# A graph-attention merge moved from a stage of its own into the loop over edge tiles

## The chip, the cores and the metric

The kernel runs on one NeuronCore of one Trainium2 chip. The metric is the device time of one execution in microseconds (us). The engines are TensorE (PE, with its weight loads PEld), VectorE (DVE), ScalarE (ACT), GpSimd (POOL) and SyncE (SP, which here only issues DMAs). Each runs its own instruction stream; semaphores order them.

## The reference, cut to what matters

Four graph layers with residual connections run over 3125 nodes of 128 features and 103125 edges, sorted by destination. The change is in the third layer, a two-head graph attention (GAT). For each edge e from src to dst and each head h:

```
z      = xl[src, h] + xr[dst, h]                  # xl = n @ Wl + bl, xr = n @ Wr + br, 128 features per head
score  = sum_f att[h, f] * leaky_relu(z[f], 0.2)
a      = exp(score - max over the edges of dst)   # softmax over the edges that end in dst
out    = sum_e a * xl[src, h]  /  (sum_e a + 1e-16)
```

The heads are then averaged and a residual projection is added. The softmax is over all edges of a destination, and these can lie in two or more edge tiles, so each tile computes with its own maximum and the tiles have to be merged: the sums of a tile are multiplied by exp(its maximum - the final or running maximum) before they are added.

## The kernel before, in words

**Tiles.** The edges lie in 202 tiles of 512, each of 4 groups (SUB) of 128. The destinations of a tile fall into a window of WIN = 20 consecutive nodes that begins at a base read at run time from `k.base_i`.

**The loop.** `attend` (L1991) serves two layers: the additive attention (`gat` false) and the GAT layer (`gat` true). `over_tiles` (L78) writes each engine's stream as a software pipeline of `(lag, stage)` pairs: in step s the engine does `stage` for tile s - lag. The ring of buffers has 8 slots in the GAT layer and 12 in the additive one; `head` rounds are written out ahead of the hardware loop, and a tail behind it. In a GAT step:

- GpSimd (L2088 to L2092) issues for tile n, once `sums_ready` says that tile n - 8 is summed, four indirect DMAs (`gather`, L894) of 128 rows of `table2` (1 KB each). Behind each gather stands a memset of a scratch tile `pause` of 128 x 280 fp16 (L905), which first waits for the memset before it. This stream is written out in full, without a hardware loop.
- TensorE does `scores` of tile s-3, `features` of s-1 (which wait for each gathered group), `turn_sums` of s-6, `turn_top` and `turn` of s-4, and `sums` of s-5.
- ScalarE does `raise_scores` (the exp) of s-3, `activate` of s-1 and `copy_sums` of s-5.
- VectorE does `tops` (the maximum per node, head and tile) of s-3, `onehots` of s, `keep_sums` of s-6 (the sums of the tile into its own strip of `k.partial`), `leaky` of s-1, `best_of_nodes` of s-4 and `edge_weights` of s-4. `best_of_nodes` (L2269) reads the window's base with `window_base` (L913, a register load from SBUF), copies the tile's maxima into `k.rows`, and keeps the maximum by node in `k.node_top` with one more instruction.
- SyncE loads the destination rows and the windows of `parts2`, two tiles at a time (L2080).

**The merge.** Behind the loop `merge_gat` (L2303) is a stage of its own, over groups of 24 tiles (`over_groups`, L1095): VectorE and GpSimd subtract the final maximum by node from each tile's maxima (L2324), ScalarE raises them (L2387), TensorE spreads the factors over 128 lanes and collects the sums of the weights by node (L2400, L2402), VectorE scales the kept sums (L2362) and adds each tile's 128 x 40 strip to `k.acc` at its window (L2374), and GpSimd adds the 2 x 20 sums of weights to `k.node_sum` (L2415). `divide_gat` (L2474) follows. Each stage ends with its semaphores cleared and a barrier.

Around the GAT layer, `project` (L561) clears `k.node_sum` and `k.node_top` just before the loop.

## Time and profile before

| | us |
|---|---|
| median of 3 runs (4847.73 to 4849.36) | 4847.86 |
| the profiled execution, its own time | 4848.75 |
| its span | 4847.0 |
| its mean granted TensorE clock, share of full speed | 0.854 |

The engines' busy shares of the whole span are PE 83%, PEld 47%, DVE 60%, ACT 36% and POOL 72%. They are averages over all layers; the stages that matter here are two stretches of the GAT layer, given as rows below. In the rows, a line number is one of the kernel before; a `q` behind an engine (POOLq, DVEq) marks its sequencer, whose register and load instructions do not count as busy. The time of TensorE's records is partly modelled.

### The profile page before, as it was taken

How to read it: one execution, taken by the hardware profiler on the slowest of the kernel's cores; microseconds unless marked ns; L12 is line 12 of the kernel's file. 1: busy time of each engine (PE TensorE's matmuls, PEld its weight loads, DVE VectorE, ACT ScalarE, POOL GpSimd, SP SyncE). 2: the span in 40 equal slices, each digit the busy share in tenths (PEclk: the TensorE clock that was granted, in tenths of full speed). 3: DMA queues.
4: the chain of work that ended last, by engine and by line, in shares of the span. 5: the costliest groups of instructions: out<-in, count | busy, mean ns of one | idle time of the engine just before them, and what ended most of it. 6: DMA issues, size and time to landing. Idle time of an engine off the chain costs nothing. (4 is left out here: it accounts for less than half of the span.)

```text
span 4847.0 us, 91319 instructions
## 1 busy us (share of the span) xinstructions
PE 4013.8 (83%) x22566; PEld 2268.5 (47%) x22566; DVE 2916.2 (60%) x8457; ACT 1759.0 (36%) x4474; POOL 3476.2 (72%) x4676
## 2 busy tenths in 40 slices
PE   3997948888888887578888888885399999999986
PEld 1344434445445445344444444442255566666652
DVE  7995043333333334656666666666688888888868
ACT  3774033344444444433333333331322222222217
POOL 0522358888888884688888888884278888888862
PEclk8998957676777767788888888886699999999999
DMA  2333522222222221333333333330066666666650
GB/s 80 86 86 97 163 68 59 56 57 57 57 57 57 57 57 33 110 100 98 99 99 99 99 99 99 99 96 9 29 101 104 104 105 105 105 104 105 104 109 14
DMA packets 377438, 402.52 MB, mean 83 GB/s; under 512 B 86457, under 2 KB 322502, under 8 KB 377030
## 3 DMA queue, kind: packets, MB, share of 16 engines
q0 software_dynamic: 151904, 198.72, 21.2%
q1 hardware_dynamic: 225382, 202.21, 14.8%
q8 instruction: 43, 0.70, 0.1%
q14 instruction: 109, 0.89, 0.1%
HBM read 312.91 MB, written 87.78 MB: 83 GB/s over the span
## 5 line engine op out<-in xcount | busy, mean ns | idle before, releaser
L1727 POOL DMA_INDIRECT sums<-gathered,idx x606 | 989.1, 1632 | 217.1 <-issue 168.5
L899 POOL DMA_INDIRECT gathered<-table,sources x952 | 912.3, 958 | 216.9 <-issue 154.7
L1589 PE MATMUL bank<-wide 128*128 128x512 bf16 x3636 | 851.4, 379 | 0.0
L2247 DVE TENSOR_REDUCE neg_raw<-bank 80x1 f32<-80x512 f32 (+1 forms) x404 | 277.5, 687 | 632.5 <-DMA dst_pair<-local_rows 192.3
L905 POOL MEMSET pause<- 128x280 f16 x1616 | 579.0, 358 | 0.4
L899 POOL DMA_INDIRECT wide<-table,sources x464 | 443.4, 956 | 106.6 <-issue 73.7
L1589 PEld LDWEIGHTS bank<-wide 128*128 128x128 bf16 x3636 | 347.7, 98 | 364.1 <-issue 1.7
L2197 ACT ACTIVATE msg<-bank,neg_top 80x512 f32<-80x512 f32 (+1 forms) x404 | 275.9, 683 | 544.5 <-DVE neg_top L2249 365.4
L1228 POOL TENSOR_TENSOR acc<-acc,msg 128x20 f32 x404 | 172.4, 427 | 350.7 <-issue 187.9
L2107 PEld LDWEIGHTS bank<-ident,gathered 128*128 128x128 f32 x1360 | 193.9, 167 | 281.0 <-issue 226.6
L2128 PE MATMUL bank<-zact,att_cells 128*80 128x512 f32 x404 | 317.5, 880 | 0.1
L2209 ACT COPY partial<-bank 32x20 f32 (+1 forms) x808 | 134.3, 166 | 480.5 <-remote 243.1
L2265 DVE COPY edge_rows<-bank 128x320 f32<-128x320 f32 (+1 forms) x404 | 183.2, 454 | 202.9 <-remote 91.4
L2240 DVE TENSOR_TENSOR zact<-zact,bank 128x512 f32<-128x512 f32 x404 | 259.5, 683 | 63.9 <-ACT zact L2189 41.5
L1175 DVE TENSOR_SCALAR gathered<-iota_c,partial 128x500 f16<-128x500 f16 x808 | 277.2, 377 | 7.9 <-PE bank L1184 6.1
L2107 PE MATMUL bank<-ident,gathered 128*128 128x128 f32 x1360 | 248.2, 321 | 40.7 <-DMA gathered<-table,sources 18.1
L2125 PE MATMUL bank<-zact,att_cells 128*32 128x512 f32 x808 | 266.9, 733 | 0.1
L1184 PE MATMUL bank<-gathered,zact 128*128 128x500 f16 x812 | 209.8, 381 | 57.2 <-ACT zact L1291 35.8
L2189 ACT ACTIVATE zact<-bank 128x512 f32<-128x512 f32 x404 | 218.8, 593 | 76.5 <-DMA window<-parts 47.9
L2138 PE MATMUL bank<-ident,msg 80*128 80x80 f32 (+1 forms) x1616 | 217.8, 264 | 33.1 <-issue 23.2
L1495 DVE TENSOR_SCALAR onehot_t<-dst_pair,iota_w,always 128x512 bf16<-128x512 bf16 x481 | 218.3, 454 | 19.5 <-DMA dst_pair<-local_rows 17.0
L2163 PE MATMUL bank<-edge_rows,gathered 128*128 128x80 f32 x1088 | 190.8, 333 | 45.8 <-issue 24.3
(407 smaller groups left out, 7803.8 us busy)
## 6 DMA issues: line engine op xcount, KB each, us to landing
zact<-in_src_flat SPq DMA_DIRECT2D x202, 192.0 KB
edge_rows<-in_attr_rows SPq DMA_DIRECT2D x202, 128.0 KB
dst_pair<-local_rows SPq DMA_DIRECT2D x177, 128.0 KB
gathered<-table,sources POOLq DMA_INDIRECT x952
dst_pair<-local_rows SPq DMA_DIRECT2D x202, 64.0 KB
counts<-wide SPq DMA_DIRECT2D x4, 3000.0 KB
counts<-fm_ab SPq DMA_DIRECT2D x4, 3000.0 KB
fm_ab<-counts SPq DMA_DIRECT2D x4, 3000.0 KB, 11.2
```

What stands on the lines that cost most here:

```text
L899: pool.indirect_dma_start(out=g[:, j, :], out_offset=None, in_=table, in_offset=bass.IndirectOffsetOnAxis(ap=mine, axis=0)).then_inc(rows_ ...
L905: pool.memset(k.pause[:, :], 0.0).then_inc(paused, 1)
L1175: hot = dve.tensor_scalar(k.cell_hot[slot][:, j, :], k.iota_c[:, :], own, None, ALU.is_equal)
L1589: pe.matmul(k.bank[b][:, :], k.split[t.two][:, c, :], k.source_hot[t.two][:, b * CHUNK:(b + 1) * CHUNK], start=first, stop=c == PARTS - 1, ...
L1727: pool.indirect_dma_start(out=k.sums[j], out_offset=bass.IndirectOffsetOnAxis(ap=k.idx[t.slot][:, j:j + 1], axis=0), in_=out_rows(t)[:, j, ...
L2107: pe.matmul(z_bank(t, h)[:, j * P:(j + 1) * P], g[:, j, h * F:(h + 1) * F], k.ident[:, :], is_transpose=True, start=(j == 0), stop=False, ...
L2125: mm = pe.matmul(score_bank(t)[own_cells(h), :], a.att[h][:, own_cells(h)], k.zact[t.two][:, h, :], start=False, stop=True, skip_group_che ...
L2128: mm = pe.matmul(score_bank(t), a.att[0][:, :], k.zact[t.two][:, 0, :], start=False, stop=True)
L2189: act.mul(k.zact[t.two][:, h, :], z_bank(t, h)[:, :], 0.2).then_inc(slope_ready, 1)
L2197: act.activation(raised(t), score_bank(t), ACT.Exp, bias=k.neg_top[lanes(t), bass.ds(t.t, 1)], accum_out=k.weight_sum[lanes(t), bass.ds(t. ...
L2240: m = dve.tensor_tensor(za, za, z_bank(t, h)[:, :], ALU.max)
L2247: dve.tensor_reduce(raw, score_bank(t), AX.X, ALU.max, negate=True).then_inc(top_found, 1)
```

## The change

1. `merge_gat` and its helpers are taken out. A class `WindowMerge` is added, and its steps are put into the GAT loop.
2. In `best_of_nodes` VectorE no longer copies the maxima to `k.rows` and takes the maximum. `note` writes (tile maximum - running best of the node) into a strip, and then updates the running best. TensorE's `turn_top` waits for this one count in place of two.
3. For every four tiles (BATCH) VectorE makes two factors per tile and node out of the noted difference d: min(-d, 0) for the old sums and min(d, 0) for the new ones (`lower`); ScalarE raises both with one exp (`raise_factors`); TensorE spreads them over the lanes and sums the weights by node (`spread_factors`, into bank 7 ahead of `turn_sums`); VectorE takes them out and scales the kept sums of the four tiles (`take`).
4. GpSimd, 17 tiles behind its own gathers, scales and adds: behind the four gathers of tile n it does for tile m = n - 17 one instruction each, `scale_rows` (2 x 20), `scale_acc` (128 x 40), `add_rows` (2 x 20), `add_acc` (128 x 40). The base of tile m's window is read into a register ahead of tile n's first gather.
5. The memset behind each gather of the GAT layer is 128 x 70 fp16 (`k.breath`); that of the additive layer stays at 280, and lies in `k.fb`.
6. Behind the last step come a tail for the last two batches, and the adds of the last six tiles on VectorE. `head` is 2 on TensorE and ScalarE and 3 on VectorE, where it was 1.
7. `node_top` and `node_sum` change partitions (32 to 33 and 0 to 1), and the two memsets that clear them change places in the list. GpSimd's stream waits once, at its start, for the bases.

```diff
-    k.node_top = k.fa[0:HEADS2, :]
-    k.sum_lanes = slice(32, 32 + HEADS2)
+    k.node_top = k.fa[32:32 + HEADS2, :]
+    k.sum_lanes = slice(0, HEADS2)
...
-    k.pause = k.sb("pause", [P, PAUSE], FP16)
+    k.pause = k.fb[:, 0:PAUSE // 2].bitcast(FP16)
+    k.breath = k.wide[:, 0, 512:512 + PAUSE // 8].bitcast(FP16)
...
+def rest(k, pool, paused, t, j, columns):
+    if t.t + j > 0:
+        pool.wait_ge(paused, t.t * SUB + j)
+    pool.memset(columns, 0.0).then_inc(paused, 1)
...
+class WindowMerge:
+    MERGED, FRONT = 17, 64
...
+    def note(self, dve, t, top, at):
+        half, i = t.slot // BATCH, t.slot % BATCH
+        best = self.k.node_top[:, bass.ds(at, WIN)]
+        wait_count(dve, self.best, t.t)
+        dve.tensor_tensor(self.raised_tops[half][:, i * WIN:(i + 1) * WIN], top, best,
+                          ALU.subtract).then_inc(self.noted, 1)
+        dve.wait_ge(self.noted, t.t + 1)
+        return dve.tensor_tensor(best, best, top, ALU.max).then_inc(self.best, 1)
+
+    def scale_acc(self, eng, m, at):
+        half, i = m % self.ring // BATCH, m % BATCH
+        wait_count(eng, self.acc_added, m)
+        w = self.k.acc[:, :, bass.ds(at, WIN)]
+        eng.tensor_tensor(w, w, self.spread[half][:, :, i * WIN:(i + 1) * WIN], ALU.mult).then_inc(self.acc_scaled, 1)
+
+    def add_acc(self, eng, m, at):
+        eng.wait_ge(self.acc_scaled, m + 1)
+        w = self.k.acc[:, :, bass.ds(at, WIN)]
+        eng.tensor_tensor(w, w, self.a.partial[:, :, m, :], ALU.add).then_inc(self.acc_added, 1)
...
+    def beside_gathers(self, pool, n, at, j):
+        m = n - self.MERGED
+        if not 0 <= m < self.k.tiles:
+            return
+        if j == 0:
+            pool.wait_ge(self.taken, self.done(m // self.ring, m % self.ring // BATCH))
+            self.scale_rows(pool, m, at)
+        elif j == 1 and m < self.pooled():
+            self.scale_acc(pool, m, at)
+        elif j == 2:
+            self.add_rows(pool, m, at)
+        elif j == 3 and m < self.pooled():
+            self.add_acc(pool, m, at)
...
+    def lower(self, dve, g, half):
+        dve.tensor_tensor(self.cell_sums[half][:, 0:n * WIN].rearrange("p (t n) -> p t n", n=WIN),
+                          k.weight_sum[:, bass.ds(first, n)].unsqueeze(2).to_broadcast([self.a.lanes, n, WIN]),
+                          place, ALU.mult)
+        dve.wait_ge(self.noted, first + n)
+        d = self.raised_tops[half][:, 0:n * WIN]
+        dve.tensor_scalar(self.factors[half][:, 0:n * WIN], d, -1.0, 0.0, ALU.mult, ALU.min)
+        dve.tensor_scalar(self.factors[half][:, wide:wide + n * WIN], d, 0.0, None,
+                          ALU.min).then_inc(self.lowered, 1)
+
+    def take(self, dve, g, half, bank, kept):
+        wait_count(dve, self.acc_scaled, first + n - self.ring)
+        dve.tensor_copy(self.spread[half][:, :, 0:n * WIN], old)
+        dve.wait_ge(kept, first + n)
+        dve.tensor_tensor(p, p, new, ALU.mult)
+        wait_count(dve, self.rows_added, first + n - self.ring)
+        dve.tensor_copy(self.row_factors[half][:, 0:n * WIN], self.factors[half][:, 0:n * WIN])
+        dve.tensor_tensor(self.row_sums[half][:, 0:n * WIN], self.factors[half][:, wide:wide + n * WIN],
+                          bank[0:self.heads, self.FRONT + 4 * wide:self.FRONT + 4 * wide + n * WIN],
+                          ALU.mult).then_inc(self.taken, 1)
...
+                if gat:
+                    pool.wait_ge(lo.limited, 1)
+                    for n in range(k.tiles + fold.MERGED):
+                        at = fold.window_of(pool, n)
+                        if n < k.tiles:
+                            t = Tile(n, n % ring, n // ring)
+                            wait_count(pool, sums_ready, n + 1 - ring)
+                            pool.sem_inc(gathers_begun, 1)
+                        for j in range(SUB):
+                            if n < k.tiles:
+                                gather_rows(k, pool, table, rows(t), rows_loaded, t, j)
+                                rest(k, pool, paused, t, j, k.breath)
+                            fold.beside_gathers(pool, n, at, j)
+                    pool.wait_ge(fold.rows_added, k.tiles)
...
-                    dve.tensor_copy(k.rows[0:heads, bass.ds(t.t * WIN, WIN)], top_bank(t)).then_inc(top_kept, 1)
-                    wait_count(dve, best, t.t)
-                    m = k.node_top[:, bass.ds(at, WIN)]
-                    dve.tensor_tensor(m, m, top_bank(t), ALU.max).then_inc(best, 1)
+                    fold.note(dve, t, top_bank(t), at)
...
-def merge_gat(k):
...
-            late=[(k.node_sum, 0.0), (k.node_top, -NEAR)])
+            late=[(k.node_top, -NEAR), (k.node_sum, 0.0)])
...
-        merge_gat(k)
```

## Rows read from the trace of the kernel before

**Rows 1.** By stretch: length; busy PE, PEld, DVE, ACT, POOL; clock; DMA share; GB/s

```profile
2017.00:3282.00 1265.00, 1057.68 (x7487) 566.11 (x7487) 765.49 (x1975) 417.88 (x995) 1057.29 (x1616) 0.87 0.35 99
3304.20:3431.50 127.30, 44.38 (x54) 11.22 (x54) 76.35 (x345) 5.18 (x9) 67.42 (x298) 0.50 0.00 1
```

**Rows 2.** Groups on POOL, 2050 to 3280 us: busy, mean ns | idle before, releasers

```profile
L899 POOL DMA_INDIRECT gathered<-table,sources x391 | 374.1, 957 | 102.7 <-issue 56.8 <-DMA wide<-table,sources 45.8 <-PE bank L2159 0.2
L905 POOL MEMSET pause<- 128x280 f16 x785 | 281.0, 358 | 0.2
L899 POOL DMA_INDIRECT h_nm<-table,sources x200 | 191.3, 957 | 47.8 <-issue 29.1 <-DMA wide<-table,sources 18.7
L899 POOL DMA_INDIRECT wide<-table,sources x194 | 185.4, 956 | 52.9 <-issue 29.8 <-DMA wide<-table,sources 23.2
```

**Rows 3.** Timeline (start, duration us, engine, line, [idle before]) around a stop of POOL

```profile
2614.91 0.95 POOL L899 DMA_INDIRECT h_nm<-table,sources  x1 [0.17 <-issue]
2615.86 0.35 POOL L905 MEMSET pause<- 128x280 f16 x1
2616.34 0.26 ACT L2203 COPY tile_rows<-bank 64x128 f32<-64x128 f32 x1 [3.78 <-DMA wide<-table,sources]
2617.09 0.96 POOL L899 DMA_INDIRECT gathered<-table,sources  x1 [0.88 <-DMA wide<-table,sources]
```

**Rows 4.** Timeline, TensorE's scores of two steps after POOL's last gather

```profile
3283.88 0.40 PE L2120 MATMUL bank<-onehot_t,far 64*64 64x512 bf16 x1
3288.32 0.40 PE L2120 MATMUL bank<-h_nm,far 64*64 64x512 bf16 x1
```

**Rows 5.** Additive layer: POOL's gathers, 800 to 1850 us; two scores after its last gather

```profile
L899 POOL DMA_INDIRECT gathered<-table,sources x465 | 445.2, 957 | 89.3 <-issue 76.0 <-PE bank L2163 7.8 <-remote 5.5
L899 POOL DMA_INDIRECT wide<-table,sources x234 | 223.6, 956 | 47.7 <-issue 38.1 <-PE bank L2163 6.0 <-remote 3.7
...
1897.12 0.41 PE L2120 MATMUL bank<-onehot_t,far 64*80 64x512 bf16 x1
1900.55 0.41 PE L2120 MATMUL bank<-zact,far 64*80 64x512 bf16 x1
```

**Rows 6.** Groups on POOL by form: the memsets whose width is nearest to 70

```profile
L347 POOL MEMSET far<- 64x80 bf16 x1 | 0.2, 155 | 0.0
L348 POOL MEMSET far<- 64x64 bf16 x1 | 0.1, 142 | 0.0
```

**Rows 7.** POOL: small two-operand instructions, a run of 24 subtracts, register loads

```profile
L1228 POOL TENSOR_TENSOR acc<-acc,msg x404: 219/226/68965, 167.7 to 610.6; 128x20 f32 x135
...
L676 POOL TENSOR_TENSOR gathered<-gathered,h_nm 128x128 f32<-128x128 f32 x1 | 0.4, 427 | 1.4 <-ACT h_nm L656 1.4
...
3306.03 5.22 POOL L2324 TENSOR_TENSOR wide<-wide,fm_ab 2x20 f32<-2x20 f32 x24 [24.45 <-issue]
...
L1191 POOLq TENSOR_LOAD <-base_i x152: 316/322/1049, 166.5 to 3429.8; - x152
```

**Rows 8.** POOL and VectorE beside each other (min/median/max ns; timeline; group; timeline)

```profile
L2324 POOL TENSOR_TENSOR wide<-wide,fm_ab x96: 210/221/808, 3306.0 to 3400.5; 2x20 f32<-2x20 f32 x48, - x48
...
3307.28 0.64 DVE L2294 TENSOR_TENSOR msg<-weight_sum,place 128x480 f32<-128x480 f32 x1
...
L2254 DVE TENSOR_SCALAR top_cells<-place,neg_top 64x20 f32<-64x20 f32 x197 | 100.7, 511 | 22.6
...
3298.55 0.24 DVE L2254 TENSOR_SCALAR top_cells<-place,neg_top 64x20 f32<-64x20 f32 x1
```

**Rows 9.** Groups on VectorE in the loop, and on VectorE and TensorE in the merge stage

```profile
L2247 DVE TENSOR_REDUCE neg_raw<-bank 64x1 f32<-64x512 f32 x198 | 136.3, 689 | 258.9 <-DMA dst_pair<-local_rows 192.3 <-PE bank L2125 66.0
...
L2362 DVE TENSOR_TENSOR partial<-partial,bank 128x480 f32<-128x480 f32 (+2 forms) x18 | 10.4, 618 | 0.3
...
L2400 PE MATMUL bank<-wide,head_row 2*128 (+2 forms) x36 | 30.2, 990 | 67.0 <-ACT wide L2387 67.0
```

**Rows 10.** Timeline, eight of the last adds of the merge stage

```profile
3427.84 2.63 DVE L2374 TENSOR_TENSOR acc<-acc,partial 128x40 f32 x8 [0.87 <-DVE partial L2362]
```

More of the change, by code:

```diff
@@ L223, in load_everything @@
     k.spot = k.sb("spot", [P, 3 * SUB])
-    k.node_top = k.fa[0:HEADS2, :]
-    k.sum_lanes = slice(32, 32 + HEADS2)
+    k.node_top = k.fa[32:32 + HEADS2, :]
+    k.sum_lanes = slice(0, HEADS2)
     k.node_sum = k.fa[k.sum_lanes, :]
-    k.rows = k.wide[:, :, :].rearrange("p a n -> p (a n)")[:, 0:T * WIN]
     k.best = k.sb("best", [1, 2 * HEADS1])
@@ L891, in gathered, with gather_rows, gather @@
         "p (j f) -> p j f", f=width)
-def gather(k, pool, table, g, gathers_begun, rows_loaded, t, paused=None):
+def gather_rows(k, pool, table, g, rows_loaded, t, j):
+    mine = k.sources[:, t.t * SUB + j:t.t * SUB + j + 1]
+    pool.indirect_dma_start(out=g[:, j, :], out_offset=None, in_=table,
+                            in_offset=bass.IndirectOffsetOnAxis(ap=mine, axis=0)
+                            ).then_inc(rows_loaded[t.slot][j], 16)
+def rest(k, pool, paused, t, j, columns):
+    if t.t + j > 0:
+        pool.wait_ge(paused, t.t * SUB + j)
+    pool.memset(columns, 0.0).then_inc(paused, 1)
+def gather(k, pool, table, g, gathers_begun, rows_loaded, t, paused):
     pool.sem_inc(gathers_begun, 1)
     for j in range(SUB):
-        mine = k.sources[:, t.t * SUB + j:t.t * SUB + j + 1]
-        pool.indirect_dma_start(out=g[:, j, :], out_offset=None, in_=table,
-                                in_offset=bass.IndirectOffsetOnAxis(ap=mine, axis=0)
-                                ).then_inc(rows_loaded[t.slot][j], 16)
-        if paused:
-            if t.t + j > 0:
-                pool.wait_ge(paused, t.t * SUB + j)
-            pool.memset(k.pause[:, :], 0.0).then_inc(paused, 1)
+        gather_rows(k, pool, table, g, rows_loaded, t, j)
+        rest(k, pool, paused, t, j, k.pause)
 def gather_sems(st, ring=RING):
@@ L2069, in attend @@
         paused = st.sem("paused")
-        cells_ready, top_turned, top_kept, best = (st.sem("cells_ready"), st.sem("top_turned"),
-                                                   st.sem("top_kept"), st.sem("best"))
+        cells_ready, top_turned = st.sem("cells_ready"), st.sem("top_turned")
         lo = Locals(st)
         merge = None if gat else RunningMerge(k, st)
+        fold = WindowMerge(k, st, ring) if gat else None
         with st.block() as block:
@@ L2088, in _ @@
             def _(pool):
-                for n in range(k.tiles):
-                    t = Tile(n, n % ring, n // ring)
-                    wait_count(pool, sums_ready, n + 1 - ring)
-                    gather(k, pool, table, rows(t), gathers_begun, rows_loaded, t, paused)
+                if gat:
[12 more added lines that the diff above has]
+                    pool.wait_ge(fold.rows_added, k.tiles)
+                else:
+                    for n in range(k.tiles):
+                        t = Tile(n, n % ring, n // ring)
+                        wait_count(pool, sums_ready, n + 1 - ring)
+                        gather(k, pool, table, rows(t), gathers_begun, rows_loaded, t, paused)
             @block.tensor
@@ L2174, in _ @@
                     over_tiles(pe, k.tiles, [(3, scores), (1, features), (6, turn_sums), (4, turn_top), (4, turn),
-                                             (5, sums)], ring=ring)
+                                             (5, sums)], head=2, ring=ring)
+                    fold.tail_spreads(pe)
                 else:
@@ L2216, in _ @@
                 if gat:
-                    over_tiles(act, k.tiles, [(3, raise_scores), (1, activate), (5, copy_sums)], ring=ring)
+                    over_tiles(act, k.tiles, [(3, raise_scores), (1, activate), (5, copy_sums)], head=2, ring=ring)
+                    fold.tail_raise(act)
                 else:
@@ L2281, in keep_sums @@
                                         "p (z c) -> p z c", z=heads)[:, :, 0:WIN]).then_inc(kept, 1)
+                    fold.behind_keeping(dve, t)
                 if gat:
                     over_tiles(dve, k.tiles, [(3, tops), (0, onehots), (6, keep_sums), (1, leaky),
-                                              (4, best_of_nodes), (4, edge_weights)], ring=ring)
+                                              (4, best_of_nodes), (4, edge_weights)], head=3, ring=ring)
+                    fold.tail_takes(dve, kept)
                 else:
```

217 lines of the change are left out of this document (109 added, 108 removed).

## The prediction, on record before the changed kernel ran

> **What bounds the kernel now.** I read four views, in this order. Busy time by stretch shows the two parts of the GAT layer that the change touches [rows 1]: 1265 us of loop with gathers (202 tiles), in which TensorE, the engine with the most work beside GpSimd, is busy 84% at a granted clock of 0.87, and 127.3 us of merge stage, in which no engine is busy more than 60% and TensorE stands at 0.50. The merge is plain serial time behind the loop: nothing else runs beside it.
>
> The groups on POOL say what paces the loop [rows 2]. 785 gathers are 196.25 tiles. Their busy time is 374.1 + 281.0 + 191.3 + 185.4 = 1031.8 us and the idle time before them 203.6 us, so a tile takes 6.295 us on POOL. Its own cadence is 4 x (0.957 gather + 0.358 memset + 0.165 from a memset to the next gather, which a row of the timeline prints as 0.17 [rows 3] and as many others as 0.16) = 5.92 us. The remaining 0.375 us per tile are stops: POOL waits for the sums of the tile 8 back. In the timeline such a stop costs 0.88 us from the end of the memset to the next gather, of which 0.165 would be there anyway, though what it waited for had come after some 0.13 us: ScalarE, released by the same sums, starts at 2616.34, the memset ended at 2616.21 [rows 3]. So a stop is mainly a restart of POOL's queue, about 0.75 us.
>
> Is it TensorE that is late? Once POOL has issued its last gather, two steps of the loop are 3288.32 - 3283.88 = 4.44 us apart [rows 4]. TensorE, ScalarE and VectorE together need 4.44 us for a tile, POOL 5.92. The loop is bound by POOL, and the stops come from TensorE's results arriving late while POOL runs. The additive layer has the same POOL stream with less on the other engines: a step without gathers takes 3.43 us, and over 699 gathers the idle time is 137.0 us, 0.124 us per tile above 4 x 0.165 [rows 5]. I read from this pair how the stops grow with the load of the others: 0.124 at 3.43/5.92 = 0.58, 0.375 at 4.44/5.92 = 0.75.
>
> **The change part by part.** All sums are made against the profiled execution, 4848.75 us (span 4847.0 and 1.75 around it); the median of the runs is 0.9 below that.
>
> *The merge stage goes.* From 3304.2 to 3431.5, -127.3 us [rows 1]. The stretch runs from the stage's first instruction to its last; the change of stages behind it stays.
>
> *POOL's stream in the loop.* Per gather the memset of 280 fp16 (0.358) becomes one of 70: between 0.142 (64 wide) and 0.155 (80 wide) [rows 6], I take 0.147. One two-operand instruction is added behind each. Not overlapped, 2 x 20 costs 0.221 [rows 8] and 128 x 40 costs 0.263, interpolated between 0.226 at 20 and 0.427 at 128 columns [rows 7], and the short gap to the one before it could be 0.06. Overlapped it costs less: 24 independent subtracts of 2 x 20 took 5.22 us, or, since a 0.81 us one is among them, (5.22 - 0.81) / 23 = 0.19 each [rows 7, 8]. All waits in this stream are for things done a gather or more before (scale at gathers 0 and 1, add at 2 and 3, the factors batches earlier), so I count none. A tile then costs on POOL at least 4 x (0.957 + 0.147 + 0.165) + 2 x 0.19 + 2 x 0.23 = 5.92, as now, and at most 5.08 + 4 x 0.06 + 2 x 0.22 + 2 x 0.263 = 6.28. I take the middle, 6.10, since the added instructions are independent of the memset but carry run-time addresses and counts. The register load of the window's base, one per tile (0.32 [rows 7]), I take as hidden: in the run of 24 subtracts such loads are issued while the engine works and leave no hole.
>
> *The stops.* The others' step grows by TensorE's part: two matmuls on 2 x 160 and one on 128 x 80 per four tiles. The merge stage did 202 tiles' worth of the first kind in 30.2 us at half clock [rows 9], twice that width is 60.4 / 202 = 0.30 per tile, 0.17 at clock 0.87, and with the third 0.2. The ratio becomes 4.64 / 6.10 = 0.76, practically today's, so I leave the stops at 0.38. The tile then takes 6.10 + 0.38 = 6.48 us against 6.295: +0.185 x 202 = +37 us.
>
> *VectorE and ScalarE in the loop.* `note` is two small instructions for two. Per four tiles `lower` adds three and `take` four: with the multiply of the kept sums at 160 columns for 480 in 0.618 (about 0.3) and the small ones at 0.2, some 1.6 us, 0.4 per tile, with the extra hand-offs 0.5. VectorE is busy 765.5 / 202 = 3.8 us per tile and idle 258.9 us before `tops` alone [rows 1, 9]; 4.3 of 6.48 leaves it off the path. If that cover were gone (VectorE in the chain of every step), the price is the 0.5 us, 100 us in all; below nothing it cannot go. ScalarE gets one small exp per four tiles and is busy a third of the time: nothing. The clears, the partitions and the moved scratch tiles: same sizes, nothing. POOL's wait for the bases at its start stands ahead of the first gather; what is queued behind it are all gathers, but the first features wait longer for the destination rows: nothing.
>
> *The tail.* Behind the last step: three small VectorE instructions at 0.2 (0.6), the exp (taken as 0.3), three matmuls (0.8: 0.99 at 480 columns [rows 9], a third of that each), two `take` (2.3), register loads (two at 0.32 [rows 7], 0.7), 12 dependent scale and add steps at 2.63 / 8 = 0.33 (4.0) [rows 10], four hand-offs at 0.3 (1.2), and POOL's row sums of the last tiles slightly behind: +11 us, between 8 and 18.
>
> **Sum:** -127.3 + 37 + 11 = -79 us: 4769.5 for the profiled run, 4769 for the median. With POOL's two ends (0 and +0.36 us per tile) 4732 and 4805.
>
> **A page against the trace.** VectorE's `top_cells` takes 0.511 us in the loop and 0.24 once POOL is idle, and one subtract of POOL took 0.808 for a median of 0.221, beginning at about the time of a 0.64 us VectorE multiply that reads two SBUF tiles [rows 8]: the two do hold each other up. The Trainium skill's page "SBUF — State Buffer", section "SBUF: two separate sides", says that VectorE and GpSimd share one pair of ports by an exclusive lock, taken by a VectorE operation with two SBUF inputs only against a GpSimd operation that reads SBUF. A memset reads nothing, the added instructions do, so by the rule the change pays more often than the memset did; it is the second rival.
>
> **Rivals.**
>
> 1. *The stops vanish.* If the added instructions let TensorE's results through as well as the longer memset did, and POOL's slower cadence lets them arrive in time, a tile costs 6.10: (6.10 - 6.295) x 202 = -39, in all 4848.7 - 127.3 - 39 + 11 = 4693. For it: 0.124 in the lighter layer. Against it: the ratio is no better than now.
> 2. *The port.* VectorE's `top_cells` (0.51 [rows 8]) and its one-hots, which I take at the same length, are 1.0 of 6.3 us per tile, so 16% of 4 instructions are hit, 0.64 per tile, each for up to 0.6 and on average 0.25 to 0.4, about 0.2 us: +43, 4812. Against it: L1228, beside a VectorE that is busy throughout, has a median of 0.226 and a minimum of 0.219 [rows 7].
> 3. *POOL's queue runs dry at every tile's first gather* (slower). The base's load and the wait for the sums both stand ahead of it; if the sequencer cannot run ahead past three instructions per gather, each tile pays a restart of 0.75 and the load's 0.32, 1.07 in place of 0.375: 6.10 + 1.07 - 6.295 = 0.875 x 202 = +177, 4909. It decides for slower from (127.3 - 11) / 202 = 0.576 us per tile. For it: 0.88 us per restart [rows 3], at every second tile already. Against it: no hole in the run of 24.
> 4. *It doesn't do what it says*: the instructions behind the gathers wait for `taken`. At gather n the batch of tile n - 17 must be taken; it is at step 12 behind the batch's first tile, and POOL runs at most some 3 steps ahead of that step count, so two steps are left. If not, the loop runs as in 3.
>
> **How the numbers follow.** Forecast (4732 to 4805) 0.50; stops gone or POOL cheaper still (below 4732) 0.15; the port or a VectorE in the chain in part (4805 to 4838) 0.15; within 0.2% (9.7 us, about what a measurement can tell from no change) 0.05; rival 3 and what lies near it 0.15. Faster 0.80, same 0.05, slower 0.15. The range 4700 to 4860 leaves out about a third of the second case and four fifths of the last, 0.17.
>
> **What the profile after would show.** The stretch between the last `keep_sums` and the next stage falls from 128 to some 11 us. On POOL, the 70-wide memset takes 0.15, the added instructions 0.19 to 0.26, gathers stay at 0.957; idle before gathers, less 4 x 0.165, is near 0.38 us per tile. The gather loop is about 1300 us long. Wrong if: the idle before a tile's first gather is near 1 us in every tile (rival 3); POOL's small instructions have means above 0.35 (rival 2); or POOL is seldom stopped and the loop is still above 6.5 us per tile, which would put VectorE in the chain.

## The result and the profile after

| | before | after |
|---|---|---|
| median of the runs, us | 4848.61 (4847.73 to 4858.41, 4 runs) | 4763.19 (4760.65 to 4772.97, 4 runs) |
| profiled execution, us | 4848.75 | 4760.65 |
| its span, us | 4847.0 | 4758.9 |
| mean granted TensorE clock | 0.854 | 0.861 |

The change makes the kernel faster: ratio 0.9819, 95% interval 0.9806 to 0.9832. The forecast was 4769 us, 6 us above the median.

Where the time went is read best by cutting both traces at the same events. The four stretches below are, in this order: the gathers of the additive layer (first to last), what lies between them and the first gather of the GAT layer, the gathers of the GAT layer, and what lies between its last gather and the first gather of the next layer (that contains the merge stage before, and the new tail after). Columns as in [rows 1]. The kernel before:

```profile
672.40:1883.40 1211.00, 1009.60 (x4123) 591.58 (x4123) 415.30 (x1254) 482.06 (x1461) 1056.05 (x1615) 0.72 0.22 58
1883.40:2016.90 133.50, 77.15 (x369) 56.76 (x368) 88.57 (x259) 65.83 (x152) 39.02 (x29) 0.74 0.18 63
2016.90:3280.30 1263.40, 1057.62 (x7487) 566.11 (x7487) 765.35 (x1974) 417.72 (x994) 1056.11 (x1615) 0.87 0.35 99
3280.30:3525.70 245.40, 111.22 (x502) 56.79 (x502) 150.81 (x553) 54.31 (x126) 84.46 (x314) 0.63 0.07 20
```

The changed kernel:

```profile
666.50:1878.50 1212.00, 1010.39 (x4135) 589.66 (x4136) 418.56 (x1258) 482.77 (x1468) 1058.11 (x1615) 0.72 0.22 58
1878.50:2006.70 128.20, 72.47 (x365) 55.09 (x363) 88.08 (x255) 64.70 (x148) 39.05 (x29) 0.74 0.19 66
2006.70:3303.90 1297.20, 1096.73 (x7766) 594.06 (x7764) 789.70 (x2303) 425.00 (x1041) 1063.87 (x2353) 0.86 0.34 97
3303.90:3437.60 133.70, 73.28 (x471) 49.83 (x472) 81.97 (x246) 50.29 (x120) 29.24 (x73) 0.73 0.13 35
```

The loop is 33.8 us longer, what follows it 111.7 shorter: -77.9 us. The other 10.2 us of the profiled pair lie outside the GAT layer: -5.9 ahead of the additive layer's gathers (they start at 672.4 and 666.5), +1.0 in them, -5.3 behind them. Is that the change? The experiments answer it, below.

The fifth number, POOL's busy time, is the surprise of the table: 1056.1 before, 1063.9 after, although 738 instructions were added (2353 for 1615). POOL in the loop, 2125 to 3300 us, for comparison with [rows 2]:

```profile
L897 POOL DMA_INDIRECT gathered<-table,sources x366 | 357.5, 977 | 97.7 <-issue 52.4 <-DMA wide<-table,sources 45.4
L897 POOL DMA_INDIRECT wide<-table,sources x184 | 180.0, 978 | 47.6 <-issue 28.0 <-DMA wide<-table,sources 19.5
L897 POOL DMA_INDIRECT h_nm<-table,sources x184 | 179.7, 977 | 50.3 <-issue 27.9 <-DMA wide<-table,sources 22.4
L906 POOL MEMSET wide<- 128x70 f16 x733 | 131.4, 179 | 0.5
L2051 POOL TENSOR_TENSOR acc<-acc,partial 128x40 f32 x184 | 52.0, 283 | 0.0
L2046 POOL TENSOR_TENSOR acc<-acc,wide 128x40 f32 x183 | 51.7, 282 | 0.0
L2057 POOL TENSOR_TENSOR fm_ab<-fm_ab,wide 2x20 f32 x183 | 39.4, 215 | 0.0
```

The memset's mean is 179 ns, not the 147 I took, and a gather's 977, not 957. But the added instruction begins 0.11 us behind the start of the memset, while that still runs (in another trace of the same kernel, shown further down, a memset at 2601.58 and the instruction at 2601.69), so of 179 ns about 110 count.

VectorE in the loop, 2050 to 3280 us (answers to [rows 8, 9]; L2107 and L2110 are the two wide instructions of `take`), and TensorE's new matmuls in the same stretch:

```profile
L2464 DVE TENSOR_REDUCE neg_raw<-bank 64x1 f32<-64x512 f32 x192 | 132.0, 688 | 167.3 <-DMA dst_pair<-local_rows 115.6 <-PE bank L2339 49.2 <-issue 0.6
...
L2471 DVE TENSOR_SCALAR top_cells<-place,neg_top 64x20 f32<-64x20 f32 x192 | 51.2, 267 | 22.0
...
L2107 DVE COPY wide<-bank 128x160 f32<-128x160 f32 x46 | 14.9, 325 | 101.3 <-DMA wide<-table,sources 51.4 <-PE bank L2385 40.5 <-POOL acc L2046 5.7
L2110 DVE TENSOR_TENSOR partial<-partial,bank 128x160 f32 (+1 forms) x46 | 14.5, 315 | 0.0
```

```profile
L2130 PE MATMUL bank<-wide,head_row 2*128 2x160 f32 x184 | 37.6, 324 | 3.6 <-ACT tile_rows L2418 3.5 <-issue 0.2
...
L2133 PE MATMUL bank<-wide,own 128*2 128x80 f32 x92 | 14.1, 235 | 0.0
```

TensorE got (37.6 + 14.1) / 184 tiles = 0.28 us per tile (46 batches of four tiles, by the count of L2107); VectorE's busy time in the loop rose by 24.3 us in all.

The 33.8 us of the loop are not spread evenly. Up to the 101st gather (tile 25) the kernel before takes 153.9 us and the changed one 164.4, 10.5 more, for 12% of the tiles; the rest takes 1109.5 and 1132.8 us, 0.13 us more per tile. In that first part POOL comes to tile 8, the first that has to wait for the sums of another tile, and stops once for long:

```profile
2062.22 0.95 POOL L897 DMA_INDIRECT gathered<-table,sources  x1 [11.51 <-PE bank L2372]
```

No gather of the kernel before waits even 2 us. The prediction has no term for this start.

The end of the stage, in three stretches (from the last gather until the last tile's sums are kept, the tail, and until the next stage's first instruction), and the two rows of the timeline that bound the last:

```profile
3303.90:3329.30 25.40, 23.70 (x209) 14.14 (x210) 18.57 (x63) 9.55 (x26) 10.82 (x47) 0.93 0.07 12
3329.30:3336.70 7.40, 2.24 (x12) 1.45 (x11) 4.26 (x24) 0.27 (x1) 2.64 (x12) 0.54 0.01 2
3336.70:3343.80 7.10, 0.00 (x0) 0.00 (x0) 0.01 (x1) 0.00 (x0) 0.00 (x0) 0.50 0.00 0
```

```profile
3336.51 0.20 DVE L2051 TENSOR_TENSOR acc<-acc,partial 128x40 f32 x1
...
3343.85 2.39 PE L2573 MATMUL bank<-ident,fm_ab 2*128 2x2 f32 x21 [12.31 <-PEq L933]
```

In the last 7.1 us every engine is idle. In the trace's full record POOL is in the drain that ends its block from 3336.21 on, for 5.78 us, so some 5.3 of the 7.1 are this drain. Before, it began that drain (7.23 us long) at 3280.2, beside its last gather and under the other engines' last tiles, and it cost nothing.

### The profile page after: what moved, and what is told of

The parts are those of the page before. It is cut to its first block and busy times, and to the rows that moved or that the text cites. A ratio compares the mean times of both kernels' runs of the same rounds, so it can differ in the third digit from the quotient of the medians.

```text
span 4758.9 us, 92081 instructions
## 1 busy us (share of the span) xinstructions
PE 4013.0 (84%) x22818; PEld 2281.2 (48%) x22818; DVE 2878.2 (60%) x8482; ACT 1762.1 (37%) x4516; POOL 3367.1 (71%) x5174
## 5 line engine op out<-in xcount | busy, mean ns | idle before, releaser
L1237 POOL TENSOR_TENSOR acc<-acc,msg 128x20 f32 x404 | 108.9, 270 | 408.3 <-issue 245.0
L906 POOL MEMSET fm_ab<- 128x280 f16 x808 | 290.5, 360 | 0.2
L1184 DVE TENSOR_SCALAR gathered<-iota_c,partial 128x500 f16<-128x500 f16 x808 | 258.8, 341 | 2.0 <-issue 1.6
L897 POOL DMA_INDIRECT h_nm<-table,sources x200 | 195.0, 975 | 55.3 <-issue 29.7
L1649 ACT COPY gathered<-bank 128x437 f32<-128x437 f32 x202 | 106.1, 525 | 336.7 <-PE bank L1624 249.6
```

The lines of the kernel that those rows point to most:

```text
L897: pool.indirect_dma_start(out=g[:, j, :], out_offset=None, in_=table, in_offset=bass.IndirectOffsetOnAxis(ap=mine, axis=0)).then_inc(rows_ ...
L906: pool.memset(columns, 0.0).then_inc(paused, 1)
L1184: hot = dve.tensor_scalar(k.cell_hot[slot][:, j, :], k.iota_c[:, :], own, None, ALU.is_equal)
```

## The experiments

They ran in three sets, each on another chip, and the kernel before took 4900, 4725 and 4909 us in them. So kernels are compared within a set, by their ratio to the kernel before in the same set. The first and the third set are close (the kernel without the added instructions took 4836 and 4833 us in them) and are read together, with care: the ratio of that kernel is 0.9872 in one and 0.9848 in the other, so a step of 0.24% between kernels of the two sets can be the sets alone. The changed kernel had 0.9795 (0.9781 to 0.9808) in the second set and 0.9820 (0.9805 to 0.9834) in the third.

| kernel | set | us | ratio to before (95%) | GAT gathers, us | POOL's stops in them, us |
|---|---|---|---|---|---|
| before | 3 | 4910 | 1.0002 (0.9994 to 1.0011) | 1295.8 | 106 |
| changed | 3 | 4818 | 0.9820 (0.9805 to 0.9834) | 1321.5 | 122 |
| TensorE's spreads twice | 3 | 4827 | 0.9836 (0.9823 to 0.9849) | 1329.3 | 130 |
| no added POOL instructions | 3 | 4833 | 0.9848 (0.9835 to 0.9862) | 1341.3 | 291 |
| memset 280 wide | 1 | 4841 | 0.9885 (0.9866 to 0.9904) | 1351.9 | 5 |
| no memset | 1 | 4827 | 0.9846 (0.9829 to 0.9862) | 1328.7 | 215 |
| before, memset 70 wide | 1 | 4935 | 1.0063 (1.0046 to 1.0080) | 1324.6 | 279 |
| changed | 2 | 4627 | 0.9795 (0.9781 to 0.9808) | 1196.2 | 1.5 |
| TensorE's spreads twice | 2 | 4630 | 0.9798 (0.9784 to 0.9811) | 1198.0 | 1.3 |
| one more VectorE instruction | 2 | 4631 | 0.9802 (0.9788 to 0.9815) | 1200.0 | 1.2 |
| rows on VectorE in the tail | 2 | 4621 | 0.9779 (0.9766 to 0.9793) | 1197.5 | 1.4 |

The last column is the length of the gathers less POOL's busy time in them less 808 x 0.165, the short gap ahead of a gather that nothing stops. By the same sum the first pair has 74 us of stops before and 100 after.

Counted in the traces, as gaps over 0.4 us ahead of a gather, the stops are these. In the first pair 95 of 0.78 us on average (over 0.165) became 102 of 0.99; in the third set 99 of 1.06 became 103 of 1.20. Most of the growth is at the start: up to the 101st gather the stops sum to 6 and 24 us in the first pair, 9 and 27 in the third set. Behind it they are 68 and 76 us, and 96 and 96. One long stop at tile 8 (10.0 to 11.5 us over the 0.165) stands in every trace of the first pair and of the first and third set in which the memset of the GAT layer is short or left out; it is absent where the memset is long, and in the second set.

**The long memset back.**

```
-    k.breath = k.wide[:, 0, 512:512 + PAUSE // 8].bitcast(FP16)
+    k.breath = k.wide[:, 0, 512:512 + PAUSE // 2].bitcast(FP16)
```

> The changed kernel with its memset behind each gather of the GAT layer back at 128 x 280 fp16; nothing else is different. Theory (the loop follows GpSimd's stream): of the 70-wide memset 0.131 us show per gather now, of one of 280 wide about 0.36, so a tile costs GpSimd 4 x 0.21 = 0.84 us more, 165 us over the loop; some of the 0.4 us of stops per tile goes. Between 4845 and 4926, I take 4900, so the move of the merge alone would have made the kernel slower. Rival (the loop follows VectorE or TensorE, and GpSimd has slack): only what the longer memset costs VectorE's instructions with two SBUF inputs comes back, about 0.25 us per tile, 4810. In both cases the mean of VectorE's top_cells (0.267 now, 0.511 before) goes back to 0.5 if it is the memset's length that holds it up; if it stays at 0.27, something else in the change did that.

Measured: 0.9885, which is 0.65% above the changed kernel of set 3, or 0.4% if the 0.24% between the sets is taken off: 20 to 32 us. The loop is POOL-bound to the last: no stops, 1351.9 us. For a kernel before of 4849 us, which the expectation had in mind, that would be 4793, below both figures. POOL's stream grew by 148 us (1213.6 for 1065.8), and of that 117 were paid by stops that went. The 4900 was wrong, and so was the sentence that the move alone would lose: with the long memset kept it still gains 1.15%. `top_cells` did not go back to 0.5 either:

```profile
L2471 DVE TENSOR_SCALAR top_cells<-place,neg_top 64x20 f32<-64x20 f32 x168 | 48.9, 291 | 19.3
```

**The kernel before with the short memset.**

```
-            pool.memset(k.pause[:, :], 0.0).then_inc(paused, 1)
+            pool.memset(k.pause[:, 0:columns], 0.0).then_inc(paused, 1)
...
-                    gather(k, pool, table, rows(t), gathers_begun, rows_loaded, t, paused)
+                    gather(k, pool, table, rows(t), gathers_begun, rows_loaded, t, paused, PAUSE // 4 if gat else PAUSE)
```

> The kernel before with the memset of the GAT layer at 70 fp16 wide and the merge still a stage of its own. Theory: GpSimd's own cadence falls from 5.92 us per tile by 4 x 0.18 to 0.21 to about 5.15, and its stops grow from 0.375 to 0.6 to 0.8 us, since the others need 4.44 us: the tile takes 5.85 in place of 6.295, 90 us less, 4760. Rival (every microsecond that GpSimd's stream gives up comes back as restarts of its queue, because TensorE's results reach it only when it pauses): 4848, no change. If the port between GpSimd and VectorE was what the long memset cost, top_cells falls from 0.511 to below 0.3 here too.

Measured: 1.0063, slower. The first experiment against my reading of the loop: POOL's stream lost 145 us (912.1, for 1056.9 in the third set's trace of before), the stops grew by 174, to 171 of 1.65 us on average. The loop row, with the clock at 0.84 for 0.86, and `top_cells`, which did fall:

```profile
2040.60:3365.20 1324.60, 1099.63 (x7470) 576.51 (x7472) 721.80 (x1969) 405.64 (x994) 912.05 (x1615) 0.84 0.33 95
```

```profile
L2254 DVE TENSOR_SCALAR top_cells<-place,neg_top 64x20 f32<-64x20 f32 x171 | 45.1, 264 | 19.8
```

What held `top_cells` up was not the memset beside it. In the steady loop of the first trace of before all 161 of its instructions above 0.4 us (of 188) begin while a gather runs on POOL, and 160 of them end with it to within 10 ns; the 24 that begin outside a gather take 0.28 us on average. Two of them from the third set's trace of before, the first inside a gather, the second inside a memset that began at 2601.56, then one from the kernel with the short memset, as far into a gather as the first:

```profile
2607.51 0.95 POOL L899 DMA_INDIRECT gathered<-table,sources  x1 [1.14 <-DMA wide<-table,sources]
2607.93 0.53 DVE L2254 TENSOR_SCALAR top_cells<-place,neg_top 64x20 f32<-64x20 f32 x1
...
2601.71 0.23 DVE L2254 TENSOR_SCALAR top_cells<-place,neg_top 64x20 f32<-64x20 f32 x1
```

```profile
2607.91 0.95 POOL L899 DMA_INDIRECT h_nm<-table,sources  x1 [1.63 <-DMA wide<-table,sources]
2608.33 0.23 DVE L2254 TENSOR_SCALAR top_cells<-place,neg_top 64x20 f32<-64x20 f32 x1
```

With the short memset 8 of 190 are above 0.4 us. Why the memset's length decides whether the gather ahead of it holds VectorE up is not shown.

So the short memset by itself loses 0.6%, and beside the added instructions it gains 0.4 to 0.65%.

**No memset where an added instruction stands.**

```
-                                rest(k, pool, paused, t, j, k.breath)
+                                if n < fold.MERGED:
+                                    rest(k, pool, paused, t, j, k.breath)
```

> The changed kernel without the memset wherever an added instruction stands behind the gather (from tile 17 on). Theory (the added instruction is breath enough): 4 x 0.131 = 0.52 us per tile of GpSimd's stream go, 0.2 come back as stops, -0.3 x 185 = -60 us, 4700. Rival (without a memset the results of TensorE get through late, and GpSimd is stopped with a full restart of 0.75 us in every tile): 6.40 - 0.52 - 0.4 + 0.9 = 6.4 us per tile, 4761 or more.

Measured: 0.9846 for 0.9820, two intervals that overlap, in two sets; the loop is 7 us longer than the changed kernel's of the third set. The theory (60 us less) fell; no gain or a small loss is what came, as the rival had it.

**No added instructions.** The four instructions of POOL became bare increments of their counts; the merged sums and the sums of weights are left out for the tiles that POOL handles.

```
-        pool.tensor_tensor(z, z, self.row_factors[half][:, i * WIN:(i + 1) * WIN],
-                           ALU.mult).then_inc(self.rows_scaled, 1)
+        pool.sem_inc(self.rows_scaled, 1)
```

> The changed kernel with the four instructions per tile that GpSimd does for the merge left out (the scaling and adding of the sums of the GAT layer for the tiles up to 196, and of the sums of weights, are left out; the counts are still posted). Theory (GpSimd paces the loop): 4 x 0.18 to 0.23 us of its stream go, stops grow by some 0.2 to 0.3, the tile takes 5.9 in place of 6.4 us, -95 us, 4665. Rival (VectorE or TensorE paces): 4760, unchanged. A GpSimd loop of 5.28 us own cadence that still takes 6.4 would be the sign of the rival.

> GpSimd's four added instructions per tile left out (the scaling and adding of the sums of the GAT layer for the tiles up to 196, and of the sums of weights), once more. Two paces: at a clock above 0.92 the loop falls from 5.92 us per tile towards 5.6 (the other engines' chain at that clock), -40 to -100 us; at 0.88 within 20 us of the changed kernel; at 0.85 not faster, and up to 30 us slower, which its first run hinted at (0.9872 on a chip where the changed kernel itself was not run). GpSimd alone paces: -0.7 us per tile on any chip, -140 us.

Measured: 0.9872 and 0.9848, the second beside the changed kernel: 15.6 us slower than with them. The loop rows of the third set say what happened: first the changed kernel, then the one without the instructions.

```profile
2039.90:3361.40 1321.50, 1122.71 (x7766) 592.50 (x7764) 781.08 (x2303) 423.28 (x1040) 1065.77 (x2354) 0.88 0.33 95
```

```profile
2038.00:3379.30 1341.30, 1130.74 (x7765) 603.20 (x7764) 775.92 (x2303) 423.60 (x1040) 916.62 (x1614) 0.85 0.32 94
```

POOL does 149 us less and stops 184 times for 1.61 us on average, the loop takes 20 us more, and TensorE, with the same 7765 matmuls, is busy 8 us longer at a clock of 0.85 for 0.88. Here GpSimd is not the pace.

**The changed kernel in another set.**

> The changed kernel itself once more, so that the others are compared with it on one chip: 0.982 of the time before. In the first four experiments the kernel before took 4900 us, not 4849, and the additive layer's gathers 1230 us in place of 1212, so traces are compared between kernels of one chip only. If the gather loop of the GAT layer is 1325 us where before takes 4900 us, the short memset and the added instructions of GpSimd were worth the differences that the four showed; if its mean TensorE clock differs too, that is named.

Measured: 4627 us, 0.9795. Its loop takes 1196 us, not 1322, with the same instructions, and there it is POOL that paces: 1.5 us of stops, and TensorE waits for gathered rows. The row of the loop, and TensorE's first use of the rows (last column), 2025 to 3150 us:

```profile
1971.90:3168.10 1196.20, 1063.48 (x7838) 558.96 (x7836) 806.93 (x2329) 432.95 (x1051) 1061.42 (x2354) 0.93 0.36 105
```

```profile
L2321 PE MATMUL bank<-ident,gathered 128*128 128x128 f32 x755 | 130.1, 290 | 58.2 <-DMA gathered<-table,sources 56.0
```

In the third set the same line waits for nothing, and TensorE waits for ScalarE's copy of the sums instead (2125 to 3250 us):

```profile
L2321 PE MATMUL bank<-ident,gathered 128*128 128x128 f32 x688 | 108.3, 296 | 8.7 <-issue 8.0
...
L2385 PE MATMUL bank<-ident,tile_rows 64*128 64x64 f32 x172 | 42.9, 249 | 65.0 <-ACT tile_rows L2418 57.0 <-issue 7.3
```

The clock column differs: 0.93 and 0.88 of 2.4 GHz over the loop. It does not order all the traces, though: the changed kernel's first one has 0.86 and a loop of 1297.2 us, the third set's 0.88 and 1321.5. The transfers are not what differs: from its start on POOL to its last packet a gather takes 2.44 us (median) in both sets. In a timeline the clock has two levels, 2.4 and 1.2 GHz. The same two groups of a tile (16 matmuls of the sums, 4 of the scores) in the second set:

```profile
2601.40 1.07 PE L2372 MATMUL bank<-h_nm,edge_rows 128*32 128x128 f32 x16
...
2602.73 1.05 PE L2339 MATMUL bank<-zact,att_cells 128*32 128x512 f32 x4
```

and in the third, in a tile at the lower level, with POOL's overlap beside it:

```profile
2599.73 1.92 PE L2372 MATMUL bank<-h_nm,edge_rows 128*32 128x128 f32 x16
...
2601.58 0.17 POOL L906 MEMSET wide<- 128x70 f16 x1
...
2601.69 0.29 POOL L2046 TENSOR_TENSOR acc<-acc,wide 128x40 f32 x1
...
2602.14 1.92 PE L2339 MATMUL bank<-zact,att_cells 128*32 128x512 f32 x4
```

**TensorE's spreads twice.**

```
-        for h in range(self.heads):
+        for h in [h for _ in range(2) for h in range(self.heads)]:
```

> The changed kernel with TensorE's two matmuls that spread the factors done twice in every batch of four tiles (36.1 us over 176 tiles in the trace, 0.205 us per tile). Theory that I now hold, since neither leaving out GpSimd's additions nor its memset made the loop shorter: the loop is paced by TensorE and by the hand-offs to and from it, and GpSimd's stream has slack. Then all of it shows: 0.205 x 202 = +41 us, a ratio of 0.9905 to before against 0.982. Rival (the theory of the prediction, GpSimd paces): 0 to +5 us, 0.982 to 0.983. A half of it would mean that the two take turns.

> TensorE's spreading matmuls twice (0.205 us per tile), once more, beside the next kernel, which takes the load off GpSimd. Two paces: at a clock above 0.92 nothing (as in the first run of it, +0.03%), at 0.88 or lower +20 to +45 us. GpSimd alone paces: nothing on any chip.

Measured: +2.4 us in the second set (0.9798 for 0.9795: nothing), +9.4 us in the third (0.9836 for 0.9820; the intervals overlap). TensorE's busy time in the loop rose by 43 and 42 us. So my second theory, that TensorE and the hand-offs pace the loop and all of it shows, fell as well: where POOL paces, nothing shows, and where it doesn't, about 8 of 42 us (with the ends of the two intervals, anything from nothing to half). The clock fell with it, 0.93 to 0.90 and 0.88 to 0.85. The row of the second set:

```profile
1978.00:3176.00 1198.00, 1106.56 (x8028) 603.92 (x8029) 791.63 (x2328) 430.51 (x1051) 1063.41 (x2354) 0.90 0.36 105
```

**One more VectorE instruction.**

```
+                    if gat:
+                        dve.tensor_tensor(k.wide[:, 0, 600:728], k.ident[:, :], k.ident[:, :], ALU.max)
```

> The changed kernel with one more VectorE instruction per tile behind the copy of the weights: the maximum of two SBUF inputs of 128 x 128 into a scratch tile that nobody reads; I put it at 0.2 to 0.35 us. Theory (VectorE has slack, as the prediction said): 0 to +10 us. Rival (VectorE is in the chain of every step): +40 to +70 us. Rival of the shared port: GpSimd's instructions become longer by the lock, means of 0.28 and 0.215 us rise above 0.3, and the time by some 20 us.

Measured: +3.7 us (0.9802 for 0.9795), for 43 us more of VectorE's busy time: it has slack in this set, as predicted. POOL's instructions hardly changed. First the changed kernel of that set, then this one:

```profile
L2046 POOL TENSOR_TENSOR acc<-acc,wide 128x40 f32 x182 | 52.6, 289 | 0.0
...
L2057 POOL TENSOR_TENSOR fm_ab<-fm_ab,wide 2x20 f32 x182 | 38.8, 213 | 0.0
```

```profile
L2046 POOL TENSOR_TENSOR acc<-acc,wide 128x40 f32 x181 | 54.8, 303 | 0.0
...
L2057 POOL TENSOR_TENSOR fm_ab<-fm_ab,wide 2x20 f32 x181 | 39.0, 216 | 0.0
```

**POOL through earlier.** VectorE scales and adds the row sums of the last six tiles as well, so that POOL ends with tile 195, and POOL waits for the bases ahead of tile 17.

```
-        if not 0 <= m < self.k.tiles:
+        if not 0 <= m < self.pooled():
...
             self.scale_acc(dve, first + i, at)
+            self.scale_rows(dve, first + i, at)
             self.add_acc(dve, first + i, at)
+            self.add_rows(dve, first + i, at)
...
-                    pool.wait_ge(lo.limited, 1)
                     for n in range(k.tiles + fold.MERGED):
+                        if n == fold.MERGED:
+                            pool.wait_ge(lo.limited, 1)
```

> The changed kernel with two edits at the ends of the GAT stage: the row sums of the last six tiles are scaled and added by VectorE, between its scale and add of the wide sums, so that GpSimd is through some 13 us earlier, and GpSimd waits for the bases ahead of tile 17 and not ahead of its first gather. Theory: in the trace of the changed kernel nothing runs for 7.1 us behind the last add, 5.78 of it while GpSimd empties its queue at the end of the block; that gap falls to about 1.3, VectorE's tail grows by 0.5 to 2, and the first gather comes up to 1.4 us earlier: -4 to -6.5 us, a ratio lower by 0.001. Rival (the emptying takes place after the last engine whatever GpSimd did before): +1, no gap closed.

Measured: 4621.16 for 4627.15 us in one set, -6.0 us, 0.9779 for 0.9795. The intervals of the two ratios overlap, but the gap in the trace, 7.7 us in the changed kernel of that set, is down to 2.2 (3201.65 to 3203.84):

```profile
3201.49 0.16 DVE L2064 TENSOR_TENSOR fm_ab<-fm_ab,wide 2x20 f32 x1
...
3203.84 0.36 PE L2577 MATMUL bank<-ident,fm_ab 2*128 2x2 f32 x2 [7.52 <-PEq L933]
```

So the drain (5.84 us here) is hidden when POOL starts it early, at 3193.4. The other edit brought nothing that the trace shows: the stretch between the two layers' gathers is 123.6 us long here, 119.5 in the changed kernel of this set. This version has the lowest median of all that were run; it beats the kernel before clearly, and the changed one by 0.13%, which the intervals don't separate.

**The kernel before and the changed one, traced in one set.**

> The kernel before, for a trace beside the three others on one chip. I now hold that the GAT loop has two paces, GpSimd's own stream (5.92 us per tile before and after, 5.22 without the added instructions, 6.69 with both them and the long memset) and the chain of the other engines, which gets longer as TensorE's granted clock falls, and that the chips differ in the second. Then, where the clock in the loop is above 0.92, GpSimd's idle time before a gather is 0.165 and the loop 1195 us; at 0.88 1263; at 0.85 about 1290.

> The changed kernel beside it. Two paces: at a clock above 0.92 its loop is as long as that of before to within 10 us; at 0.88 about 35 us longer, at 0.85 30 to 45 longer, since the other engines' chain grew by TensorE's 0.28 us per tile and by the batches' hand-offs. If GpSimd's added instructions were what made the loop 34 us longer, the difference would be the same on any chip.

Measured: 4909.7 and 4817.8 us, ratio 0.9820. The loop of before took 1295.8 us at a clock of 0.86 (1290 were expected at 0.85, 1263 at 0.88), the changed one's is 25.7 us longer (30 to 45 were expected): 8.6 of them up to the 101st gather, 17.1 or 0.10 us per tile behind it, and what follows it is 112.9 us shorter (249.9 to 137.0). The first stretch ends the question of the 10 us outside the GAT layer. In the trace of before that was read for the prediction, the first of POOL's 404 adds in an early stage (L1228 of [rows 7]) took 68.97 us; here, in the same kernel, the longest took 0.80, and the additive layer's gathers start at 666.9, not 672.4. The kernel with the long memset, whose code there is the changed kernel's, has one of 69.00 us again and starts them at 673.8. The row of before in the third set, then the long memset's (shortest, median and longest in ns):

```profile
L1228 POOL TENSOR_TENSOR acc<-acc,msg x404: 219/226/800, 168.1 to 605.1; 128x20 f32 x135
```

```profile
L1237 POOL TENSOR_TENSOR acc<-acc,msg x404: 219/226/68997, 168.3 to 611.8; 128x20 f32 x135
```

So these 5.9 us go with one instruction of 69 us, which 2 of the 14 traces have, one of before and one of the changed code; they are not the change's. What makes it so long was not tried. The stretch between the layers varies too: 137.0 to 140.4 us in the three traces of the third set with the changed kernel's code in it, 142.6 in before.

## Why the prediction was right, point by point

The median came out 6 us below the forecast. The stage that goes and the tail were sized well; for the loop the total was nearly right (+34 us for +37) because two terms missed in opposite directions, and that is luck.

- **The merge stage goes, the tail comes** (-127.3 and +11, so -116.3): behind the last gather the traces show -111.7 and -112.9. The tail was mis-sized by 3 to 5 us; its list lacked POOL's drain, some 5.3 of the 7.1 idle us. The tail proper was 7.4 us, below the 11.
- **POOL's stream** (+0.18 us per tile, +37 us): mis-sized, the step that failed by most. In the steady loop POOL is busy 0.11 us per tile more (936.3 us over 175.5 tiles for 937.9 over 179.5), and the first 17 tiles, which have only the short memset, are 0.7 us cheaper each. Together +8 us (1056.1 to 1063.9), near the lower bound of the sum.
- **The stops** (0.38 us per tile, unchanged): 74 us before and 100 after, 26 more, of which 18 lie up to the 101st gather. Behind it they are 0.38 and 0.43 us per tile, so "unchanged" was nearly right there, and in the third set right (0.54 and 0.54; its growth of 17 us is all at the start). What was missing is the start. The two errors, 29 and 26 us, cancel: +33.8 measured, +37 forecast. That a stop is mainly a restart of some 0.75 us fits the first trace (0.78 on average), but not the third set (1.06) or the kernels with a shorter POOL stream (1.65 and 1.61): there most of a stop is a wait for the others.
- **"The loop is bound by POOL"** holds only in part. In the second set, with 0.93 in the clock column, POOL was hardly ever stopped and added work on TensorE or VectorE did not show. In the other sets, at 0.88 and below, 149 us less on POOL did not shorten the loop. The step behind it failed: the 4.44 us that the others need for a tile [rows 4] were read where the clock is higher than in the loop, which the prediction did not look at. The stretch of that view, with 1.00 in the clock column against 0.87 in [rows 1]:

```profile
3281.00:3299.00 18.00, 16.67 (x155) 9.69 (x155) 13.32 (x40) 7.69 (x20) 0.58 (x2) 1.00 0.06 13
```

  TensorE's busy time alone is 1057.7 / 202 = 5.24 us per tile in [rows 1], so the others' step could not have been 4.44.
- **VectorE and ScalarE cost nothing**: shown for VectorE by the extra instruction, in the set where POOL paces; at the lower clock it wasn't tried. VectorE's own time rose by 0.12 us per tile, not 0.4, since `top_cells` became 0.24 us cheaper.
- **TensorE's part** (0.2 us per tile): 0.28. Doubling most of it cost 2 and 9 us for 43 and 42 us of work, so a quarter of such work or less shows, by the medians.
- **Rival 1**, the stops vanish: in the second set they did. There the ratio was 0.9795, not the 0.968 of the rival's 4693 us, since the kernel before was faster there too (4725 us; it was not traced there, so its stops are not known).
- **Rival 2**, the port: POOL's added instructions have means of 215 and 283 ns, below the 350 that would have shown it, and one more VectorE instruction with two SBUF inputs raised one of them by 14 ns and the time by 3.7 us. The prediction held the long memset against the added instructions by a rule of the Trainium skill. The Trainium skill's page "SBUF — State Buffer", section "SBUF: two separate sides", says that a VectorE operation with two SBUF inputs takes the shared ports only against a GpSimd operation that reads SBUF, and one in a 2-port mode against any. No run here tells which of the two `top_cells` is, or tests the rule on a memset: what holds `top_cells` in the long cases is a gather, which takes its row numbers from the SBUF tile `sources`. What the prediction drew from the rule, that the change pays more often, did not come: the mean of `top_cells` is 469 ns before and 264 with the shorter memset alone, 291 with the long memset and the added instructions, and with the short memset and them 281 in the third set and 367 in the second (the faster one). So neither the memset's length nor the added instructions settle it; when the two engines' instructions meet must matter too, and that is argued, not shown.
- **Rivals 3 and 4**, a restart at every tile, or waits for `taken`: the stops of 100 us are 0.50 per tile, not 1.07, and the added instructions show next to no idle time ahead of them (0.0 in the rows above).

What stays open: why the other engines' chain gets longer when POOL's stream gets shorter. It did in the kernels with the short memset in before and without the added instructions, and by 7 us, which two sets do not separate, in the one with no memset; each has a TensorE clock in the loop lower by 0.02 to 0.03 than its pair of the third set, and TensorE's busy time rose by 8 to 29 us for the same work. Whether the clock is the cause or follows from the other order of work isn't settled, nor is what stops POOL at tile 8 for 11 us. Nor was the kernel without the added instructions run where the clock is high; the two-paces theory expects a gain there, and that was not tried. Nor was before traced there. An estimate: 4725.0 - 4627.2 us is 97.9 less in all, and with 112 to 113 less behind the loop, the loop grew by some 14 us in that set.

## What to carry to other kernels

When an engine looks like the pace of a loop because it is busiest, take work off it before pricing what is added: if its stops grow by as much as its stream shrinks, it isn't. Read another engine's step at the clock of the loop, not of the quiet stretch behind it. And when a stage goes, ask what its time had hidden: GpSimd, having issued gathers, took 5.0 to 8.4 us here to end its block, so let it finish before the others do.

## What the runs showed of the hardware that was not expected

- The same kernel took 4725 to 4909 us in different sets (3.9%), that is on different chips. For the changed kernel nearly all of the difference lies in the two layers with these gathers: they took 1186 and 1196 us in one set, 1234 and 1322 in another. That is 172 of the 197 us between their traces. The next layer's indirect DMAs took 1173.4 and 1172.5. The clock differed in the GAT loop (0.93 and 0.88), a gather's 2.44 us did not; what makes the clock differ was not tried.
- A two-operand POOL instruction behind the short memset starts 0.11 us after the memset does, before it ends, so of the memset's 0.18 us 0.11 count. A gather starts 0.16 us behind the end of what is ahead of it.
- A gather on POOL can hold VectorE's `top_cells` until the gather ends: 0.53 us for 0.23. Of 188 tiles it did so in 160 of the kernel before, and 8 of 190 were above 0.4 us when only the memset behind each gather was cut from 280 to 70 columns.
- POOL's drain at the end of a block with gathers took 5.8 us and was exposed only because POOL finished last.
